# Halving the products of a 31-tap filter by taking two windows at a time, and parting the expert weight loads in two

## The reference

```python
q, k, v = (silu(causal_dwconv(xn @ W, conv_w)) for each)       # 4 taps, 4 heads x 32
delta_out = delta_rule_chunkwise(q, k, v, sigmoid(xn @ W_b))   # chunks of 32 steps, a state per head
fir_s = causal_dwconv(v, fir_short_w)                          # 3 taps
fir_l = causal_dwconv(v, fir_long_w)                           # 31 taps, one filter per channel
hid = gelu(concat(xn, fir_s, fir_l, delta_out) @ W_fuse1 + b)
gates = ...(hid @ W_fuse2 + b)                                 # sigmoid and softmax over paths
o = rmsnorm(g0 * fir_s + g1 * fir_l + g2 * delta_out + g3 * v) @ W_o
# experts: top 2 of 8, F = 256
y = (silu(z @ Wg + bg) * (z @ Wl + bl)) @ W3 + b3,  z = (x @ W1 + b1) * (x @ W2 + b2)
```

## Time and profile before

| | |
|---|---|
| runs (3) | 944.1 us median, 938.4 to 949.76 |
| the profiled execution | 942.49 us, span 940.5 us, mean granted TensorE clock 0.803 |
| busy: TensorE matmul, weight load | 689.9 us (73%), 533.5 us (57%) |
| busy: DVE, ACT, GpSimd | 564.0 us (60%), 296.7 us (32%), 489.4 us (52%) |
| instructions | 34845, of them 15324 matmuls and 15324 weight loads |

### The profile page before, as it was taken

How to read it: one execution, slowest core, us unless ns; L and a number is a source line. 1 busy time by engine, 2 the same in 40 slices (tenths; PEclk the granted TensorE clock), 3 DMA queues, 4 the chain that set the end, 5 groups by cost and what they waited for, 6 DMA issues and landing times.

```text
span 940.5 us, 34845 instructions
## 1 busy us (share of the span) xinstructions
PE 689.9 (73%) x15324; PEld 533.5 (57%) x15324; DVE 564.0 (60%) x1233; ACT 296.7 (32%) x511; POOL 489.4 (52%) x546
## 2 busy tenths in 40 slices
PE   3437788869876887869787787778777778896551
PEld 2226667647665665656566565556556555665431
DVE  6899786457665459834675375634674377235353
ACT  2210053334322443324332253233332343223020
POOL 3721377863765468765647365753655353423211
PEclk9965587877987889897887797687896798799575
DMA  8302132131124113140221223221232211301243
GB/s 306 127 31 85 36 83 91 62 88 39 42 52 138 20 57 105 30 138 13 71 88 29 78 29 89 79 78 14 79 82 26 78 63 17 84 14 61 98 139 112
DMA packets 61493, 69.35 MB, mean 74 GB/s; under 512 B 39712, under 2 KB 44832, under 8 KB 61216
## 3 DMA queue, kind: packets, MB, share of 16 engines
q0 software_dynamic: 9200, 34.78, 12.9%
q1 hardware_dynamic: 51712, 30.42, 11.3%
q10 hardware_dynamic: 432, 1.94, 0.5%
HBM read 47.45 MB, written 19.66 MB: 71 GB/s over the span
## 4 chain that ended last, share of the span: by engine, by line
PE 36%; issue 14%; DVE 12%; DMA 6%; POOL 4%; SPq 3%; ACT 2%; DVEq 0%; POOLq 0%; ACTq 0%
PE ps_shared L1575 6%; PE ps_shared L1734 5%; PE ps_g L1571 5%; PE ps_x L1571 4%; PE ps_shared L1796 3%; PE ps_l L1571 3%; PE ps_shared L1713 3%; DMA system_d<-masked 3%; SPq L835 2%; PE ps_shared L1571 2%; PE ps_shared L1580 2%; DVE solve_prod L1415 2%; DMA w_mid<-y_d 2%; POOL xs L987 1%; DVE comb L1560 1%
## 5 line engine op out<-in xcount | busy, mean ns | idle before, releaser
L987 POOL DMA_INDIRECT xs<-xn_d,owner_i x92 | 94.7, 1029 | 78.6 <-DVE put_i L1326 27.0
L1005 POOL DMA_INDIRECT y_d<-work,put_i x92 | 93.0, 1011 | 58.0 <-DVE work L1552 30.8
L1571 PE MATMUL ps_g<-z,w_mid 128*128 128x512 f32 x276 | 97.7, 503 | 20.8 <-POOL z L1039 12.9
L1571 PE MATMUL ps_x<-xr,w_up 128*128 128x512 f32 x276 | 97.2, 467 | 6.9 <-issue 3.5
L1734 PE MATMUL ps_shared<-head_vs,taps 32*32 32x16 f32 x4096 | 62.7, 200 | 41.1 <-issue 39.8
L1571 PEld LDWEIGHTS ps_g<-z,w_mid 128*128 128x128 f32 x276 | 64.9, 245 | 42.2 <-issue 27.6
L1734 PEld LDWEIGHTS ps_shared<-head_vs,taps 32*32 32x32 f32 x4096 | 55.9, 131 | 49.3 <-issue 48.0
L1571 PE MATMUL ps_l<-z,w_mid 128*128 128x512 f32 x276 | 82.2, 435 | 1.1 <-DVE work L1547 1.1
L1542 DVE SCALAR_TENSOR_TENSOR work<-ps_g,w_tile,work 128x512 f32<-128x512 f32 x46 | 34.3, 746 | 74.9 <-ACT work L1203 74.9
L1039 POOL TENSOR_TENSOR z<-work,z 128x512 fp32r<-128x512 f32 x46 | 60.2, 1308 | 30.6 <-ACT z L1197 30.1
L1343 DVE SCALAR_TENSOR_TENSOR acc<-pre,late_sb,acc 128x512 f32<-128x512 f32 x72 | 62.8, 872 | 9.2 <-ACT acc L1098 8.2
(11 more groups left out here) (252 smaller groups left out, 1456.2 us busy)
## 6 DMA issues: line engine op xcount, KB each, us to landing
xa_d<-xr SPq DMA_DIRECT2D x8, 512.0 KB, 2.6
xa<-xa_d SPq DMA_DIRECT2D x8, 512.0 KB, 3.7
w_mid<-y_d SPq DMA_DIRECT2D x16, 256.0 KB, 3.4
system_d<-masked SPq DMA_DIRECT2D x8, 256.0 KB
x_res<-hidden SPq DMA_DIRECT2D x8, 256.0 KB
part_d<-x_res SPq DMA_DIRECT2D x8, 256.0 KB
comb<-part_d SPq DMA_DIRECT2D x8, 256.0 KB, 2.8
out<-comb SPq DMA_DIRECT2D x8, 256.0 KB, 2.1
```

Source lines behind the costliest of these rows:

```text
L987: pool.indirect_dma_start(xs[par][:, c, :], None, xn_d.rearrange("w p (c d) -> (w p c) d", c=CPW), bass.IndirectOffsetOnAxis(owner_i[:, w ...
L1005: pool.indirect_dma_start(y_d, bass.IndirectOffsetOnAxis(put_i[:, w * CPW + c:w * CPW + c + 1], 0), y_sb[par][:, c * D:(c + 1) * D], None) ...
L1571: made = pe.matmul(to, weights[a], x[b], start=start and n == 0, stop=stop and n == 2)
```

## The change

It has two parts, and a new order that follows from them.

1. **Filter.** A product of `fir_l` takes two windows: 32 columns in place of 16, so 4 pairs of windows (`PAIRS`) with 256 products each in place of 8 windows. A pair's result needs two banks, each with 16 of the 32 channels. ACT copies each bank to SBUF (`fir_l_half`, into `fir_steps`, which takes the place of the routing tables), and DVE transposes from there, a window at a time. `head_vs` is one tensor with both windows; the copy in front is made once a pair. The filter of windows 2v and 2v+1 can begin only after `v_T` of window 2v+1.
2. **Weights.** The gather is parted: `load_split` (1536 columns, one buffer `w_split`, after `split_up` and `split_mid` of the tile before) and `load_plain` (392 columns, two buffers, after `y_out` of tile t - 2). `w_up` has two buffers, so `split_up` of tile t waits for the `up2` of tile t - 2 and no longer for that of t - 1.
3. **Order.** `FLOW` has other costs for some steps and `PULL` other priorities, so the lists of all engines change.

```diff
-    def long_filters(w):
-        yield need(("v_T", w, 0))
+    def long_filters():
+        yield need(("place", 0, 0))
+        for v in range(PAIRS):
+            yield need(("v_T", 2 * v + 1, 0))
+            for half in range(2):
+                bk = yield TAKE
+                for k in range(PARTS // 2):
+                    yield "fir_l", v, PARTS // 2 * half + k, bk
+                if v:
+                    yield need(("fir_l_out", 2 * v - 1, 0))
+                yield "fir_l_half", v, half, bk
+                leave(bk, "fir_l_half", 2 * v + half + 1)
+    def filtered(w):
+        yield need(("fir_l_half", w // 2, 1))
+        if w >= 1:
+            yield need(("fir_l_T", w - 1, 0))
-        bk = yield TAKE
-        for k in range(PARTS):
-            yield "fir_l", w, k, bk
-        yield "fir_l_out", w, 0, bk
-        leave(bk, "fir_l", w + 1)
+        yield "fir_l_out", w, 0, None
...
-                                made = pe.matmul(filtered[rows, :, e], taps[rows, e, last, :], head_vs[par][rows, at:at + RUNS, e],
+                                made = pe.matmul(by_half[rows, :, e % KH], taps[rows, e, last, :], head_vs[rows, at:at + 2 * RUNS, e],
...
+                elif name == "fir_l_half":
+                    act.wait_ge(S["fir_l_ps"], 2 * w + i + 1)
+                    act.wait_ge(S["placed"], 1)
+                    if w:
+                        act.wait_ge(S["fir_l"], 2 * w)
+                    act.activation(fir_steps[:, :, i * KH:(i + 1) * KH], ps[:, :].rearrange("p (r e) -> p r e", e=KH),
+                                   ACT.Copy).then_inc(S["fir_l_half"], 1)
...
-                    dve.transpose(runs(fir_l), ps[:, :].rearrange("p (r e) -> p r e", e=HD)).then_inc(S["fir_l"], 1)
+                    dve.transpose(runs(fir_l), fir_steps[:, par * RUNS:(par + 1) * RUNS, :]).then_inc(S["fir_l"], 1)
...
+                elif name == "load_split":
+                    pool.wait_ge(S["placed"], 1)
+                    if w:
+                        pool.wait_ge(S["up_low"], w)
+                        pool.wait_ge(S["mid_low"], w)
+                    pool.indirect_dma_start(w_split[:, :], None, expert_split,
+                                            bass.IndirectOffsetOnAxis(row_i[:, w:w + 1], 0)).then_inc(S["in_split"], 16)
-                elif name == "load_w":
+                elif name == "load_plain":
                     if w < 2:
                         pool.wait_ge(S["placed"], 1)
                     else:
                         pool.wait_ge(S["y_sb"], w - 1)
-                    pool.indirect_dma_start(w_tile[par][:, :], None, expert_rows,
-                                            bass.IndirectOffsetOnAxis(row_i[:, w:w + 1], 0)).then_inc(S[f"in_w{par}"], 16)
+                    pool.indirect_dma_start(w_plain[par][:, :], None, expert_plain,
+                                            bass.IndirectOffsetOnAxis(row_i[:, w:w + 1], 0)).then_inc(S[f"in_plain{par}"], 16)
...
-        w_tile = [sb(f"w_tile{n}", P, WIDTH) for n in range(2)]
-        w_up = sb("w_up", P, 2 * UPS, dt=FR)
+        w_split = sb("w_split", P, SPLIT)
+        w_plain = [sb(f"w_plain{n}", P, PLAIN) for n in range(2)]
+        w_up = [sb(f"w_up{n}", P, 2 * UPS, dt=FR) for n in range(2)]
...
-    "v_act": [[(POOL_, 2.1)]], "v_T": [[(DVE_, 0.7)]], "v_b": [[(DVE_, 0.7)]], "fir_l": [[(PE_, 1.9)]], "fir_l_out": [[(DVE_, 0.7)]],
+    "v_act": [[(POOL_, 2.1)]], "v_T": [[(DVE_, 0.7)]], "v_b": [[(DVE_, 0.7)]], "fir_l": [[(PE_, 3.2)]], "fir_l_half": [[(ACT_, 0.65)]], "fir_l_out": [[(DVE_, 0.7)]],
```

More of the change, by code:

```diff
@@ L108 @@
     "o_T": [[(PE_, 1.0)]], "o_T_out": [[(ACT_, 0.6)]],
-    "out": [[(PE_, 1.2)]], "store": [[(DVE_, 0.7)], [(SP_, 0.5, 2.5)]],
+    "out": [[(PE_, 2.0)]], "store": [[(DVE_, 0.7)], [(SP_, 0.5, 2.5)]],
 }
[L111 to L121, removed]
@@ new lines @@
+PULL = {"beta_T": -100, "blend": 100, "choose": -200, "combine": -400, "conv": -150, "conv0": 150, "count": 300,
+        "delta_again": 350, "down": -300, "fetch": -100, "fir": 500, "fir_l": -400, "fir_l_T": -50, "fir_l_out": 150,
+        "fir_s_T": 200, "full": -100, "fuse": 300, "fuse2": 450, "gate_T": 50, "gates": 350, "gelu": 100, "hid": 100,
+        "inv": -400, "inverse_out": -50, "k_T": -50, "ln": -300, "load_plain": 200, "load_x": -50, "load_xs": -450,
+        "load_xt": 50, "masks": 350, "masks0": -600, "mid_g": 350, "mid_l": -250, "mix_s": -350, "mix_v": 300,
+        "norm": -300, "o": -200, "o_T_out": -100, "on_state": -250, "out": 600, "owned": 200, "place": 600, "q_T": -150,
+        "rank": -600, "rms": -350, "solve_mul": -500, "solve_sum": -100, "split": -50, "split_mid": 50,
+        "split_qkv": -50, "split_up": -50, "sumsq": -300, "swish": 500, "times": 300, "turn": 100, "u_adj": 500,
+        "up1": -300, "up2": 300, "v_T": 350, "v_act": -100, "v_again_T": -100, "v_b": -200, "w_T": -200, "w_T_out": 450,
+        "x_res": 300, "xn_out": 100, "y_out": -150, "z": 50, "zeros": -350}
@@ L122 @@
+LEAN = {}
 SOLVE_LOADS = 2 * SEQS
@@ L413, in expert_turns, with expert_weights, expert_splits @@
             yield from turn(WINDOWS + t)
-    def expert_splits(kind, behind):
+    def expert_weights():
+        yield need(("place", 0, 0))
         for t in range(TILES):
-            yield need(("load_w", t, 0))
             if t:
-                yield need((behind, t - 1, FJ - 1))
+                yield need(("split_up", t - 1, 0), ("split_mid", t - 1, 0))
+            yield "load_split", t, 0, None
+    def expert_splits(kind, ring, behind):
+        for t in range(TILES):
+            yield need(("load_split", t, 0))
+            if t >= ring:
+                yield need((behind, t - ring, FJ - 1))
             yield kind, t, 0, None
@@ L424, in expert_ups @@
             t, j = divmod(g, FJ)
-            yield need(("split", WINDOWS + t, 0), ("split_up", t, 0))
+            yield need(("split", WINDOWS + t, 0), ("split_up", t, 0), ("load_plain", t, 0))
             if g >= 2:
@@ L492, in schedule @@
                windows(triangles), windows(attend), *(expert_loads("load_xs", n, lambda t: ("turn", WINDOWS + t, 0)) for n in range(2)),
-               *(expert_loads("load_w", n, lambda t: ("y_out", t, 0)) for n in range(2)),
-               expert_splits("split_up", "up2"), expert_splits("split_mid", "mid_l"), expert_turns(), expert_ups(), expert_zs(), expert_mids(), expert_gates(), expert_downs(), expert_puts(0), expert_puts(1),
-               windows(fuse), windows(mix), windows(finish), windows(combine), windows(filters), windows(long_filters)]
+               *(expert_loads("load_plain", n, lambda t: ("y_out", t, 0)) for n in range(2)), expert_weights(),
+               expert_splits("split_up", 2, "up2"), expert_splits("split_mid", 1, "mid_l"), expert_turns(), expert_ups(), expert_zs(), expert_mids(), expert_gates(), expert_downs(), expert_puts(0), expert_puts(1),
+               windows(fuse), windows(mix), windows(finish), windows(combine), windows(filters), long_filters(), windows(filtered)]
     ready = [0.0] * len(streams)
@@ L544, in schedule @@
                 engine = groups[n][1][0][0][0]
-                starts.append((max(ready[n], clock[engine]), tails.get(last[n], 0.0) + PULL.get(last[n][0], 0.0), n))
+                starts.append((max(ready[n], clock[engine]), tails.get(last[n], 0.0) + PULL.get(last[n][0], 0.0) + LEAN.get(last[n][0], 0.0) * last[n][1], n))
         best = None
@@ L582, with layer @@
 SIGNALS += [f"in_xa{n}" for n in range(3)]
-SIGNALS += [f"{k}{n}" for k in ("in_xa_d", "in_w", "in_xs", "in_y_d", "in_comb", "in_y12") for n in range(2)]
-def layer(nc, hidden, early, late, expert_rows, taps_in, out):
+SIGNALS += [f"{k}{n}" for k in ("in_xa_d", "in_plain", "in_xs", "in_y_d", "in_comb", "in_y12") for n in range(2)]
+def layer(nc, hidden, early, late, expert_split, expert_plain, taps_in, out):
     ctx = ExitStack()
@@ L658, in layer @@
         head_v = sb("head_v", P, RUNS, HD)
-        head_vs = [sb(f"head_vs{n}", P, SEQS + RUNS, HD) for n in range(2)]
+        head_vs = sb("head_vs", P, SEQS + 2 * RUNS, HD)
+        window_v = [head_vs[:, SEQS + n * RUNS:SEQS + (n + 1) * RUNS, :] for n in range(2)]
         masks = sb("masks", P, CPW, 2, SEQS, CHUNK)
@@ L1765, in _ @@
                         pe.wait_ge(S["up1"], g)
-                    product(ps_x1[:, :], [up_of(part, 0, i) for part in range(2)], x).then_inc(S["x1"], 1)
+                    product(ps_x1[:, :], [up_of(w, part, 0, i) for part in range(2)], x).then_inc(S["x1"], 1)
                 elif name == "up2":
@@ L1771, in _ @@
                         pe.wait_ge(S["z"], g)
-                    product(ps_x2[:, :], [up_of(part, 1, i) for part in range(2)], x).then_inc(S["x2"], 1)
+                    product(ps_x2[:, :], [up_of(w, part, 1, i) for part in range(2)], x).then_inc(S["x2"], 1)
                 elif name == "mid_g":
```

96 lines of the change are left out of this document (52 added, 44 removed).

## The result

The changed kernel takes 901.52 us (median of 4, 901.38 to 909.65) against 943.41 (938.4 to 949.76): ratio 0.9574, 95% interval 0.9495 to 0.9653, 42 us less. The profiled execution has a span of 899.9 us and a mean granted clock of 0.812.

The account below looks back on a forecast made before the run. TensorE's own list was taken to set most of the pace. Filter matmuls and gaps save 46 us, times 0.65 is 30, less 3 for the loads: 27 us off 942.5, 917 by the median; range 895 to 943.

Parts of the forecast that it names:

- forecast: Main case for the whole kernel: filter time and gaps shrink and part passes, 27 us less, 917 us; chance 0.51.
- all of it passes: Rival: all filter time and gaps saved reach the end and the clock holds more often, 896 us; chance 0.13.
- The filter's matmuls: On TensorE: 2048 products of 32 columns at 18 ns, 37 us busy, 26 us saved (0 to 36).
- The gaps: TensorE's standing before filter matmuls, read as waits for instruction packets: 16 packets fewer, 20 us saved (0 to 30).
- The passage: Share of TensorE's 46 us saving that reaches the end of the run: 0.65, giving 30 us.
- The pairing's wait: Even window's filter waits for the odd window's `v_T`; 16 us of work fits 22.5 us of cover, costed at nothing.
- The parted loads: GpSimd: 23 more indirect DMAs, 33 us more work, one us in thirteen on the path; 3 us cost in all.
- GpSimd's list becomes the bound: Rival: `load_split` holds up GpSimd's list, low halves of z come late, 15 us slower, 959 us; chance 0.12.
- The clock: TensorE's granted clock after filter parts: fewer gaps may spare slow stretches; 0 in the sum, up to 10 us in the range.
- The end: Last window's filter parts and last recurrence: this end can give back about 12 us, not all 23.
- the gaps stay: Rival: gaps not due to instructions, 930 us; or strided columns cost double, 934 us; chance 0.14 together.
- freed time did turn into waits: Rival: triangular-system steps and the tile's own sequence hold the pace, TensorE stands instead, 942 us; chance 0.10.

Follow-up runs that it names:

- half filter: Kernel before, its lists kept, filter products for the chunk before left out (2048 matmuls of 16 columns, not 4096): 903.98 us, ratio 0.9535.
- loads alone: Kernel before plus the parted weight loads, filter unpaired: 954.48 us (1.0092) on its own tables, 925.74 us (0.9774) on the changed kernel's.
- filter alone: Kernel before plus the paired filter, weight loads unparted: 903.20 us (0.9526) on its own tables, 925.96 us (0.9794) on the changed kernel's.
- tables alone: Kernel before with the cost and priority tables of the changed kernel, nothing else: 968.93 us, ratio 1.0241.
- pair with equal lists: Changed kernel, 901.52 us, and the same lists with each 32-column filter product made as two of 16, 951.33 us.
- doubled filter: Changed kernel with each 32-column filter product made as two of 16 in the same place of the list: 951.33 us, ratio 1.0063.

## Why the prediction was right

The forecast was 917, 27 us less; 42 us less came, within the range of 895 to 943. The mechanism is the one forecast, fewer small instructions and fewer gaps before them; the case "forecast" with a share of "all of it passes" describes it.

- *The filter's matmuls.* 18 ns each forecast, 17.1 measured, 37 against 35.0 us. The choice by the row of contiguous 32 columns was right, and the half filter shows why: columns up to 32 are nearly free. Of the floor of 25 ns (the Trainium skill, "TensorE: Matmul & The Clock Gate", "Back-to-back issue gap") nothing shows here; 51 us would have been half again too much. That the width does not matter among such narrow ones does hold, from 16 to 32.
- *The gaps.* 20 us forecast, with a bound of 30; 31.8 measured. The rule by packets is right for the filter: on the old tables pairing took the gaps from 39.8 to 19.7* us, and from 28.2 to 7.9 beside the parted loads. The other 12 us came with the parted loads, whose effect on the gaps the forecast put at nothing. They did not help the time, since the loads alone are slower. The instruction queue brought 105 packets, as forecast. The rule that block crossings are mostly hidden (the Trainium skill, "Runtime: NRT & Kernel Launch", "Instruction fetch mechanics") fits the changed kernel, with 8.0 + 12.2 us of gaps left for 105 packets. For the kernel before, with 39.8 + 36.8 us for 121, it does not fit where small matmuls stand together.
- *The passage.* This is the mis-sized term: 0.65 forecast. On the tables that the forecast started from, pairing took 27.7 + 20.3 = 48 us off TensorE's filter time and gaps beside the parted loads (the forecast had 46), and 47 of them came out at the end, 0.98. With half of the filter left out it was 0.78; filter alone against tables alone, 43 of 49.8, it was 0.86. Over the whole change it looks like 42 of 59.5 us, 0.70, because the 59.5 hold the 12 us of gaps that brought nothing and the 42 are net of what the loads cost. The passage depends on the list: filter and loads against loads alone on the new tables it was 19 to 24 of some 50* us.
- *The pairing's wait.* Costed at nothing, which was right for the time by wrong reasoning: I took the filter to fit into 22 us of cover. It did not; fuse of window 0 came 48 us later than before. That is luck. The likely reason that the delay had no price is that the recurrence doesn't need fuse and the rest of the list went on without it; what is shown is that the half filter with the old places is no faster.
- *The parted loads.* Forecast a cost of 3 us. On the old tables it was 8 us alone, and 4 beside the filter, within the intervals: the sign is right and the size low. The passage for GpSimd was wrong: one us in thirteen holds for the kernel before, but 16.5 to 22 us hang on the second gather. I had this as the rival "GpSimd's list becomes the bound"; GpSimd got its share of the chain, 26%, and the price stayed below what would have turned the result. A shorter list of TensorE is not needed for that share: it is 20% with the tables alone.
- *The clock.* Put at 0, with 10 us in the range. In the pair with equal lists some 6 us of other matmuls' time came back, at 0.85 for 0.83 over the same stretch. The whole-run clock of the doubled filter ranges from 0.781 to 0.833 over its ten executions, so one trace of each does not show that the gaps moved it.
- *The end.* It gave back nothing beyond what the whole gave: 44 us from the last `delta_T` for 42.

So the 15 us beyond the forecast are mostly the passage: on the old tables the filter's part was sized right on TensorE and brought 44 us at the end for the 30 put. The loads cost a little more than put. The new order, which the forecast left out, was worth some 2 us once both parts were in (0.9574 for 0.9593), less than the intervals. The rival "the gaps stay" is out by the doubled filter and by the count through the trace. Some of the freed time did turn into waits, those for GpSimd.

## What to carry to other kernels

Where a fixed list has bursts of small matmuls, count instructions, not columns, and ask how fast each block of 256 is worked off. In these runs a product of twice the width at the same count of instructions was nearly free up to 32 columns, and the gap before a burst was part of its price. Price new work on the engine that is next on the chain by the chain after the change, not by the one before. And when a change comes with new planner tables, run parts and tables apart, on both sets: each part alone on the new tables looked like 43 us, and on the old ones one of them made the kernel slower.

## What the runs showed of the hardware that was not expected

- TensorE's instructions come in packets of 16 KB: 105 for 26552 matmuls and weight loads, 121 for 30648, 253 each; counted with TensorE's semaphore instructions, a block has 256. In runs of small matmuls gaps of more than 1 us, up to 4.6, open only at one place in 256 instructions, whichever line is there, and end 1.2 to 1.6 us after a packet landed: all 34 of the kernel before, all 10 of the changed one, all 27 with the doubled filter. They follow blocks that are worked off fast, 24 of 26 under 2.5 us against none of 53 over 5 us. No run took the packets' delay away.
- A 32x32 fp32 matmul takes 15.3 to 16.4 ns with 16 strided columns and 17.1 ns with 32 (busy over count), four heads side by side.
- An order alone, the same work on each engine, moved the time by 2.4% and GpSimd's share of the chain from 4% to 20%.
